# A four-stage transformer block on one core: another order of the steps on VectorE and GpSimd

## The reference

```python
x = x + tanh(g_xattn[0]) * L0_xattn(layernorm(x), ctx, ctx)       # attention by a divergence, then an MLP
x = x + tanh(g_ffn[0])   * L0_ffn(layernorm(x))                   # fp8-quantised linear layer
x = x + tanh(g_xattn[1]) * L1_xattn(layernorm(x), ctx, ctx, mask) # 16 heads of 16, softmax, projection
x = x + tanh(g_ffn[1])   * L1_ffn(layernorm(x))                   # r + 0.5*(silu(ln(r)@w1+b1)@w2+b2)
```

## Time and profile before

| what | value |
|---|---|
| median of 3 runs | 1606.79 us (1606.21 to 1613.41) |
| the profiled execution | 1611.25 us, its span 1609.4 us |
| mean granted TensorE clock | 0.963 |
| busy: PE, PEld, DVE, ACT, POOL | 92%, 71%, 82%, 71%, 64% |

### The profile page before, as it was taken

The page is one execution under the profiler, slowest core; times in us unless marked ns, Lnnn a source line. Parts: engine busy times, 40 slices in busy tenths (PEclk is TensorE's granted clock), DMA queues, the critical chain, the costliest instruction groups (busy, mean ns, idle before and its releaser), DMA issues.

```text
span 1609.4 us, 42630 instructions
## 1 busy us (share of the span) xinstructions
PE 1483.6 (92%) x14155; PEld 1141.0 (71%) x14155; DVE 1318.3 (82%) x3187; ACT 1135.4 (71%) x2057; POOL 1030.6 (64%) x1392
## 2 busy tenths in 40 slices
PE   3899999999999974478999999999999999999997
PEld 2788888888888863245676677777777777767666
DVE  4798888888888876787888889898988888898732
ACT  7798888888888743265666666676666666666664
POOL 4688888888888743324456565666656565665445
PEclk8899999999999995588999999999999999999999
DMA  6322322322322002422222232233322332233100
GB/s 225 107 73 67 96 67 65 97 65 74 89 65 72 1 1 85 139 83 72 78 81 75 83 88 79 79 87 85 87 81 78 84 86 78 82 83 86 56 17 21
DMA packets 197690, 125.45 MB, mean 78 GB/s; under 512 B 44400, under 2 KB 196848, under 8 KB 197360
## 3 DMA queue, kind: packets, MB, share of 16 engines
q1 hardware_dynamic: 197616, 124.48, 26.7%
HBM read 92.69 MB, written 25.17 MB: 73 GB/s over the span
## 4 chain that ended last, share of the span: by engine, by line
PE 46%; SPq 6%; DMA 3%; DVE 2%; issue 2%; POOL 1%; ACT 1%; POOLq 0%
PE b_bank L1837 27%; PE b_bank L1912 6%; PE b_scoreT L1894 4%; PE b_score L1877 4%; PE b_bank L1845 2%; SPq L1293 2%; DMA b_nmT<-b_nm 1%; SPq L1282 1%; PE b_bank L1989 1%; SPq L1309 1%; PE b_bank L1927 1%; DMA b_yT<-b_y 1%; SPq L1318 1%; DVE b_nm L1653 1%; SPq L1326 1%
## 5 line engine op out<-in xcount | busy, mean ns | idle before, releaser
L1471 ACT ACTIVATE b_E<-b_scoreT 128x1024 f32<-128x1024 f32 x256 | 262.2, 1024 | 151.4 <-PE b_scoreT L1894 151.1
L1653 DVE TENSOR_REDUCE b_nm<-b_score 128x4 bf16<-128x1024 f32 x256 | 313.3, 1224 | 57.4 <-PE b_score L1877 51.2
L31 ACT ACT_TABLE_LOAD x157 | 201.4, 1283 | 18.6 <-PEq L1059 15.2
L1837 PE MATMUL b_bank<-f,b_YT 128*128 128x256 bf16 x1536 | 193.0, 277 | 4.7 <-POOL b_YT L1404 4.6
L890 PE MATMUL bank<-hT,W1T 128*128 128x256 bf16 x1536 | 183.3, 273 | 2.4 <-DVE hT L706 1.6
L1837 PE MATMUL b_bank<-b_hT,f 128*128 128x256 bf16 x1536 | 183.4, 273 | 0.8 <-DVE X L1749 0.8
L890 PE MATMUL bank<-W2T,G 128*128 128x256 bf16 x1024 | 171.0, 272 | 6.7 <-DVE GT L780 6.2
L1837 PEld LDWEIGHTS b_bank<-f,b_YT 128*128 128x128 bf16 x1536 | 144.7, 99 | 40.8 <-issue 19.3
L1837 PEld LDWEIGHTS b_bank<-b_hT,f 128*128 128x128 bf16 x1536 | 147.7, 98 | 30.4 <-issue 12.6
L890 PEld LDWEIGHTS bank<-hT,W1T 128*128 128x128 bf16 x1536 | 147.9, 98 | 27.8 <-ACT G L549 4.1
L1388 POOL TENSOR_TENSOR b_v<-b_v,b_e 128x512 f32<-128x512 f32 x32 | 40.7, 1270 | 194.1 <-DVE b_e L1734 194.1
(11 more groups left out here) (222 smaller groups left out, 3537.1 us busy)
## 6 DMA issues: line engine op xcount, KB each, us to landing
b_Q<-q_dram SPq DMA_DIRECT2D x192, 64.0 KB, 2.5
b_K<-k_dram SPq DMA_DIRECT2D x192, 64.0 KB, 2.7
xin<-in_x SPq DMA_DIRECT2D x32, 256.0 KB, 3.1
ctxn<-in_ctx SPq DMA_DIRECT2D x32, 256.0 KB, 2.8
mask_in<-in_mask SPq DMA_DIRECT2D x32, 256.0 KB, 3.0
X<-in_x SPq DMA_DIRECT2D x32, 256.0 KB, 4.0
ctxt<-in_ctxT SPq DMA_DIRECT2D x32, 256.0 KB, 4.2
b_ctxt<-in_ctxT SPq DMA_DIRECT2D x32, 256.0 KB, 2.8
```

The source lines that it names most:

```text
L31: act.add_instruction(mybir.InstLoadActFuncSet(name=nc.get_next_instruction_name(), act_func_set_id=which, ins=[], outs=[]))
L1471: nc.scalar.activation(E[:, pair:pair + 2], scoreT_ps[:, :, :, :], ACT.Exp).then_inc(sig["E"], 1)
L1653: nc.vector.tensor_reduce(pair, score_ps[:, :, :, :], AX.X, ALU.max, negate=True).then_inc(sig["nm"], 1)
L1837: last = nc.tensor.matmul(out_tile, lhs(i, k), rhs(j, k), start=start and k == chunks[0] and (i, j) == TERMS[0], stop=stop and k == chunks ...
```

## The change

Only the order of steps on VectorE and GpSimd changes; each instruction does what it did. In VectorE's list for one iteration:

- `scaled`, `binades`, `mlp_columns`, `magic` and `base` stand together behind `attended(1)`, between `maxima(0)` and `maxima(1)`. Before, `scaled` was ahead of `attended(0)`, and the others stood between `maxima(3)` and `maxima(4)`.
- `statistics_3`, until now the end of `attention_update`, is a step behind `maxima(5)`; `statistics_2` is behind `maxima(6)`, ahead of `result`.
- `mlp_normalised` is one of the last steps, for stage `o`, instead of the first one of the next iteration, for stage `h` (the same item); `attention_normalised` and `mask_bias` follow it.
- `attended_low` and `maxima(3)` change places.

On GpSimd `inverse_std_2` moves ahead of `silu_parts(h, 0)`.

```diff
                 if o:
                     inverse_std_3()
-                if h:
-                    silu_parts(h, 0)
                 if f:
                     inverse_std_2()
                 if h:
+                    silu_parts(h, 0)
                     silu_parts(h, 1)
...
-                if h:
-                    mlp_normalised()
-                if n:
-                    scaled()
                 if o:
                     attended(0)
                 if m:
                     maxima(0)
                 if q:
                     normalised_low()
+                if o:
+                    attended(1)
...
-                if o:
-                    attended(1)
+                if n:
+                    scaled()
+                    binades()
+                if h:
+                    mlp_columns()
+                if n:
+                    magic()
+                if h:
+                    base()
                 if m:
                     maxima(1)
...
                 if m:
                     maxima(5)
+                if o:
+                    statistics_3()
+                if m:
                     maxima(6)
+                if f:
+                    statistics_2()
                 if w:
                     result()
+                if m:
+                    maxima(7)
+                if o:
+                    mlp_normalised()
                 if f:
-                    statistics_2()
+                    attention_normalised()
                 if q:
                     mask_bias()
-                if m:
-                    maxima(7)
-                if f:
-                    attention_normalised()
```

More of the change, by code:

```diff
@@ L1629, in mlp_normalised @@
                 def mlp_normalised():
-                    dve.wait_ge(sig["rs3"], done(h))
-                    if (due := done(h, back=1)) is not None:
+                    dve.wait_ge(sig["rs3"], done(o))
+                    if (due := done(o, back=1)) is not None:
                         dve.wait_ge(sig["hT_mm"], due)
                     for t in range(T):
-                        last = nc.vector.tensor_scalar(hn[:, t, :], Xb(h, t), mv3[:, t, 0:1], rh3[:, t:t + 1], ALU.subtract,
+                        last = nc.vector.tensor_scalar(hn[:, t, :], Xb(o, t), mv3[:, t, 0:1], rh3[:, t:t + 1], ALU.subtract,
                                                        ALU.mult)
@@ L1750, in attention_update, with statistics_3 @@
                                                    ALU.add).then_inc(sig["x3"], 1)
+                def statistics_3():
                     dve.wait_ge(sig["x3"], done(o))
@@ L1785, in iteration @@
                     queries_low()
+                if m:
+                    maxima(3)
                 if o:
                     attended_low()
-                if m:
[L1789 to L1793, removed]
                 if at_iteration(half, parity, 1):
@@ L1797, in iteration @@
                     quantised_update()
[L1798 to L1801, removed]
                 if m:
```

## The result

The changed kernel takes 1819.97 us (median of 4 runs, 1816.42 to 1829.24) where the kernel before took 1607.02 beside it: the ratio is 1.1324, with a 95% interval of 1.127 to 1.1378. It is slower by 13%, 12 us above the 1808 us of the prediction and inside its range. The profiled execution took 1822.80 us, its span is 1821.0 us, the mean granted clock 0.918 against 0.963.

The account below looks back on a forecast made before the run. TensorE, busy 473 of 473 us in mid-phase, was taken as the bound. 26 x (5.8 + 1.7) = 195, + 9 - 3 = +201 on 1611.25 gives 1812, less 4.46 to the median: 1808 us; 8-in-10 range 1700 to 1850.

Parts of the forecast that it names:

- The place and the chain: On VectorE, `scaled` starts at 1130.46 behind `attended(1)`; the moved steps follow and the second reduction ends at 1138.12.
- The size of the stall: TensorE's `scores(2)` starts at about 1138.15, not at 1132.36: 5.8 us of stall in each full iteration.
- the lower bound: At `scores(2)`, the order with nothing else in the way costs 2.1 us; as a rival 1661 us, chance 0.12.
- Who is held: Beside GpSimd's work, VectorE's moved instructions wait, ending 0.15 us (small ones 0.03) behind GpSimd's, which keep their durations.
- exclusion for a whole instruction: Rival for the moved steps: held instructions pay their full 0.40 us, 1.6 us more per iteration, 1850 us; chance 0.08.
- The clock: On TensorE after each stall, one stretch of about 3.4 us at half the clock: 1.7 us lost per iteration.
- The sum: Over the whole kernel, 195 + 9 - 3 = +201 us on the profiled execution, predicting 1808 us.
- the very term of the sum: In the 26 iterations with `n`, `m` and `h` together: 26 x (5.8 + 1.7) = 195 us.
- on which I had put 3: Waits for the transposes of b_yT between 800 and 900 us vanish in longer iterations: 3 us less.
- The iterations before the 26: In the three first iterations with `m`, TensorE follows VectorE's chain, whose length stays the same: 0 us.
- my inner range: The forecast's own range, 1765 to 1845 us, from a stall of 5.2 to 6.4 us and clock loss 1 to 2.7.
- What costs nothing: Moved statistics, normalisations, GpSimd's exchange and earlier `rounded`: no cost outside the five steps ahead of the second reduction.

Follow-up runs that it names:

- the runs with GpSimd cut: Changed kernel and kernel before, both with most columns of GpSimd's later `silu_parts` and bias additions left out and `rounded` waiting for `base`: 1672.88 and 1601.31 us.
- the run with the early `magic` in the kernel before: Kernel before with `binades` and `magic` directly behind `maxima(3)`, `mlp_columns` and `base` behind `quantised_update`: 1634.74 us, ratio 1.016.
- the run with the stall filled: Changed kernel with the product of queries made four times more than needed on TensorE, same result: 1798.03 us.
- half a group: Kernel before with only `mlp_columns` and `base` moved ahead of `maxima(1)`: 1696.50 us.

## Why the prediction was right

*The place and the chain.* Right, nearly step for step. Counted from the beginning of the iteration, `scaled` was reckoned to start at 3.83 us and starts at 3.86; `binades` to end at 6.24 and ends at 6.32; the first of `mlp_columns` 7.36, measured 7.35; `magic` 8.84, measured 8.97; the end of the second reduction 11.49, measured 11.70.

*The size of the stall.* 5.8 us reckoned, 6.1 measured; the runs with GpSimd cut share it into 2.0 of order (2.1 reckoned as the lower bound) and 4.1 of collisions. So the lower bound is a part of the stall. The end of the second reduction is 0.2 us later than reckoned. 0.13 of it is `magic`: I had read 0.15 us behind GpSimd's instruction from rows of 128x256 and used it for b_e, of 128x512, too, which ends 0.28 behind. The rest is `base`: its first instruction got in before GpSimd's b_v, which then took 1.36 (alone 1.27), and the second one was late with it.

*Who is held.* VectorE, as the rows said: in the iteration shown it ends 0.15 behind GpSimd's instruction with those of 128x256 (b_v, X), 0.28 with those of 128x512 (b_e) and 0.02 with b_tg, while GpSimd's own stay within 0.1 of what they take alone. It isn't always so: in the run with the early `magic` in the kernel before, GpSimd's b_y began while the held update of X was still at work, and took 1.50 us for 1.26. Taken literally, the Trainium skill's exclusion for a whole instruction ("SBUF — State Buffer", "Who interferes with whom") would have added 1.6 us; the trace agrees with the exclusion, not with that price.

*The clock.* 1.7 us reckoned, 1.92 measured by the run with the stall filled. I had taken one stretch of 3.4 us at half the clock; there are 6.8 us, part of them inside the stall: the stretch from 1163.4 begins 3.7 us before `scores(2)` starts at 1167.06, the one from 1129.3 only 1.4 before it starts in its iteration:

```profile
1130.68 0.61 PE L1880 MATMUL b_score<-b_K,b_Q 48*128 48x256 bf16 x4 [6.09 <-DVE b_nm L1652]
```

That twice the stretch, partly hidden, costs about what one stretch in the open would have is luck. The mean granted clock in the middle is 0.90, not the 0.95 that I named.

*The sum.* From the first reduction of the fourth item to that of the thirtieth, the 26 iterations, 732.0 us became 927.2 (729.68 to 1461.70, and 731.13 to 1658.35): 195 more, the very term of the sum. That it fits to the microsecond is partly luck: 26 x (6.1 + 1.9) is 208, and about 13 us come back, on which I had put 3. Some 9 of them are waits that the first of these iterations held before (29.6 us against 27.8) and that have gone. The other 5 are the first of these iterations in the changed kernel, which takes 29.45 us and not 35.85, less what some of the next ones take more. Stage `w` has no item in it yet, so GpSimd has no `silu_parts(w, ...)` and no bias of the MLP to make beside the group, and the same group passes in 3.4 us (733.49 to 736.93), held only in `base`, by `rounded`:

```profile
733.49 0.73 DVE L1715 TENSOR_SCALAR b_v<-X,mu,rsq 128x256 f32<-128x256 f32 x2
734.25 0.43 DVE L1721 TENSOR_SCALAR b_e<-b_v 128x512 int32<-128x512 int32 x1
734.60 0.22 DVE L1639 TENSOR_SCALAR b_tg<-b_rs,gate 128x2 f32<-128x2 f32 x1
735.34 1.67 DVE L1727 TENSOR_SCALAR X<-X,b_up,b_dn 128x256 f32<-128x256 f32 x2
```
```profile
738.21 0.39 PE L1880 MATMUL b_score<-b_K,b_Q 48*128 48x256 bf16 x4 [2.74 <-DVE b_nm L1652]
```

So the collisions show in the changed kernel itself: the wait is 2.74 us without GpSimd's work beside the group and 6.1 with it. I had counted this iteration like the others.

The iterations before the 26 gave 1.4 us (0 reckoned), those behind them 14.9 (9 reckoned). The stall in the latter was no longer than reckoned, 7.7 us in three rounds; TensorE's waits for the maxima from 1655 us on are

```profile
PE b_score L1880 <- DVE b_nm L1652: 7.7, 3, 3.0
```

What the sum lacks there is a term for the clock. In these three iterations the mean granted clock is 0.90, 0.95 and 0.87, where the kernel before has 1.00, 1.00 and 0.97; TensorE's waits for b_hT also grew, from 0.2 to 3.1 us. How the rest divides between the two wasn't measured. `mlp_columns` has a third instruction that I took for free; in two of the three iterations it was held for a whole GpSimd instruction, in the place of the others:

```profile
1661.37 1.12 DVE L1642 SCALAR_TENSOR_TENSOR b_dn<-b_mv,b_tg 128x2 f32<-128x2 f32 x1
```

The limits of my inner range were added up wrongly: a stall of 5.2 to 6.4 us and a clock loss of 1 to 2.7 give 1774 to 1849, not 1765 to 1845. The measured time lies inside both.

*What costs nothing.* Right: the statistics, the normalisations, the mask and GpSimd's exchange are neither a loss nor, beyond 0.2%, a gain.

## What to carry to other kernels

In a list that an engine takes in strict order, an instruction's price is set by the deadline of the one behind it: 0.30 us of margin stood here against 2.7 us of moved work, while 1.4 us of idle time were left at the place from which work was taken. Before VectorE's float32 steps between SBUF tiles are moved, look at what GpSimd does at the new place, instruction by instruction: 2.7 us of work became 6.6 beside a busy GpSimd. And a regular wait on TensorE is dearer than it looks where the granted clock falls behind it, so much that useless products in the gap made the kernel faster.

## What the runs showed of the hardware that I had not expected

A longer stall isn't always followed by a longer slow stretch. With 6.1 us of wait in each iteration 1.92 us were lost to the clock; with 1.98 (GpSimd cut) the iteration took 30.69 us against 27.87 in its base, over the same 18 iterations, so 0.84; with 2.85 (half a group) 0.36. Most iterations of that last run took 30.7 to 30.8 us, without any loss, and a few about 32.3. When it falls and when not stays open here.

An instruction of 128x2 elements can be held as long as a far larger one (1.10 us for b_tg, alone 0.22; 0.95 for a b_e of 128x512, alone 0.42). And b_dn, which has two inputs in SBUF, took 0.15 in each of the 26 iterations, where it starts at the seam of two GpSimd instructions or beside none, and 1.12 where it started 0.05 us after one.
